# Attention in chunks with a carried state: another order of the chunk's work on four engines, and a state term in four matmuls instead of six

## What is computed

```python
x  = L0_attn_x                                   # 4 x 1024 x 256, float32
xn = layernorm(x)
gammas = 1.0 - 2.0 ** (-5.0 - arange(16))
q, k, v = (xn @ W.T for W in (W_q, W_k, W_v))    # 16 heads of 16
decay = where(i >= j, gammas ** (i - j), 0)
attn  = einsum('bihd,bjhd->bhij', q, k) * decay / 4
y     = einsum('bhij,bjhd->bihd', attn, v)       # then a norm per head, and W_o
...
out = x + attention(xn) + ffn(xn)                # ffn: 8 experts, the best 2 of each token
```

## Time and profile before

| | us |
|---|---|
| median of 3 runs | 962.76 (961.16 to 964.6) |
| the profiled execution, device time | 965.13 |
| its span, first to last instruction | 963.1 |
| mean granted TensorE clock, as a share of full speed | 0.955 |
| busy over the span: TensorE, VectorE, ScalarE, GpSimd | 857.8, 763.6, 573.5, 561.7 |

### The profile page before, as it was taken

The page is one execution under the profiler, slowest core; times in us unless marked ns, Lnnn a source line. Parts: engine busy times, 40 slices in busy tenths (PEclk is TensorE's granted clock), DMA queues, the critical chain, the costliest instruction groups (busy, mean ns, idle before and its releaser), DMA issues.

```text
span 963.1 us, 22162 instructions
## 1 busy us (share of the span) xinstructions
PE 857.8 (89%) x7040; PEld 805.8 (84%) x7040; DVE 763.6 (79%) x1156; ACT 573.5 (60%) x1009; POOL 561.7 (58%) x409
## 2 busy tenths in 40 slices
PE   3949889889888888799899999999999999999865
PEld 1438778778777777699899999999999999999855
DVE  5687877777777778847888888888888888888476
ACT  3824444444443444338677787777777777777541
POOL 2217565666666666535566666666666666666254
PEclk9959999999999999959999999999999999999877
DMA  9923333333333333355577677777677777777487
GB/s 304 354 86 97 92 86 85 80 80 82 85 81 84 85 80 82 85 226 175 191 239 226 227 235 232 227 229 231 228 231 229 230 229 229 229 229 221 140 263 254
DMA packets 106249, 170.49 MB, mean 177 GB/s; under 512 B 30768, under 2 KB 77232, under 8 KB 96240
## 3 DMA queue, kind: packets, MB, share of 16 engines
q1 hardware_dynamic: 99408, 151.49, 51.4%
q0 software_dynamic: 6816, 18.69, 5.2%
HBM read 115.88 MB, written 33.18 MB: 155 GB/s over the span
## 4 chain that ended last, share of the span: by engine, by line
PE 60%; DVE 21%; issue 8%; ACT 3%; DMA 3%; another core or an unknown queue 2%; DVEq 1%; POOL 1%; SPq 0%; ACTq 0%
PE ps L706 23%; PE ps L904 22%; DVE arena_r L1142 5%; PE ps L794 5%; DVE arena_f L1149 4%; PE ps L779 2%; PE ps L889 2%; DMA arena_f<-pair_rows 2%; PE ps L819 1%; PE ps L724 1%; PE ps L762 1%; DVE arena_f L1173 1%; DVE y_stats L1165 1%; ACT arena_r L567 1%
## 5 line engine op out<-in xcount | busy, mean ns | idle before, releaser
L706 PE MATMUL ps<-arena_r 128*128 128x256 f32 (+1 forms) x2256 | 291.7, 285 | 20.1 <-DVE arena_f L1173 18.0
L706 PEld LDWEIGHTS ps<-arena_r 128*128 128x128 f32 x2256 | 277.6, 193 | 26.3 <-issue 24.2
L486 POOL TENSOR_TENSOR arena_r<-arena_f,arena_r 128x2048 fp32r<-128x2048 f32 x39 | 191.5, 4909 | 134.3 <-ACT arena_r L560 134.3
L904 PE MATMUL ps<-arena_r 128*128 128x256 f32 x1872 | 234.0, 285 | 0.8 <-DVE gn_t L1298 0.8
L904 PEld LDWEIGHTS ps<-arena_r 128*128 128x128 f32 x1872 | 230.3, 194 | 0.9 <-issue 0.9
L1235 DVE TENSOR_SCALAR arena_f<-arena_f 128x256 f32<-128x256 f32 x78 | 156.0, 2040 | 1.4
L560 ACT ACTIVATE arena_r<-arena_f 128x2048 fp32r<-128x2048 f32 x78 | 145.5, 1919 | 1.6 <-PE ps L706 1.6
L467 POOL TENSOR_TENSOR arena_r<-arena_f,arena_r 128x512 fp32r<-128x512 f32 x64 | 93.7, 1475 | 57.4 <-ACT arena_r L567 55.7
L819 PE MATMUL ps<-arena_r 128*128 128x128 f32 x1024 | 126.1, 284 | 0.0
L819 PEld LDWEIGHTS ps<-arena_r 128*128 128x128 f32 x1024 | 123.5, 201 | 0.0
L639 ACT ACTIVATE arena_f<-ps,arena_f 128x256 f32<-128x256 f32 x156 | 65.0, 471 | 94.3 <-PE ps L904 73.2
(11 more groups left out here) (141 smaller groups left out, 1060.2 us busy)
## 6 DMA issues: line engine op xcount, KB each, us to landing
arena_f<-w SPq DMA_DIRECT2D x78, 1024.0 KB, 6.0
xs_rows<-spare_rows SPq DMA_DIRECT2D x39, 258.0 KB, 3.3
arena_f<-xs_rows SPq DMA_DIRECT2D x39, 258.0 KB, 2.9
arena_r<-arena_r SPq DMA_DIRECT2D x256, 32.0 KB
pair_chunk<-xn SPq DMA_DIRECT2D x32, 256.0 KB, 2.6
arena_f<-pair_rows SPq DMA_DIRECT2D x16, 512.0 KB, 5.4
arena_f<-b SPq DMA_DIRECT2D x39, 128.0 KB, 4.5
xn<-x SPq DMA_DIRECT2D x8, 512.0 KB, 8.8
```

The lines of the kernel that those rows point to most:

```text
L486: nc.gpsimd.tensor_tensor(w1_r[par][:, 1], w1_raw[par], w1_r[par][:, 0].bitcast(F32), ALU.subtract).then_inc(s["w1_l"], 1)
L706: last = pe.matmul(out_ap, lhs(a), rhs(b), start=start and n == 0, stop=stop and n == 2, **kw)
L904: last = pe.matmul(ps[:, 2 + hp, o * SLOT:(o + 1) * SLOT], w1_r[par][:, a, at:at + P], xs_r[:, b, k * SLOT:(k + 1) * SLOT], start=(m == 0 ...
```

## The change

TensorE begins its round with the scores. The transposes of keys and queries, which were at the head, come after the state sums and the x transposes, and the projection is split in two with the y transposes between. VectorE's `transposed_low(i+1)` moves from the head to behind the third mask, the token low part to between masks, the state sum goes ahead of them; output sum and statistics change places, and so do the values' low part and `keys_and_queries`. ScalarE begins with the transposed tokens; the keys' copy comes before the fourth score's. GpSimd's low part of the state moves from behind the scores and keys to the head. Masks 1 and 3 now wait too, for VectorE's own low part. `across` is written with four matmuls: the high part of the queries by both parts of the state at once (256 columns, into both column sets), and the low part by the high part. SyncE is as it was.

```diff
             def step(i, par):            # GpSimd
+                if within(i - 1, NT):
+
+                    pool.wait_ge(s["st_h"], i)
+                    nc.gpsimd.tensor_tensor(state_r[:, 1], state_f.rearrange("p c i -> p (c i)"),
+                                            state_r[:, 0].bitcast(F32), ALU.subtract).then_inc(s["st_l"], 1)
                 if within(i, NT):
                     for g in (0, 2):
...
-                if within(i - 1, NT):
-
-                    pool.wait_ge(s["st_h"], i)
-                    nc.gpsimd.tensor_tensor(state_r[:, 1], state_f.rearrange("p c i -> p (c i)"),
-                                            state_r[:, 0].bitcast(F32), ALU.subtract).then_inc(s["st_l"], 1)
                 if within(i + 2, NT):
                     chunk_scatter(i + 2, par)
...
             def chunk(i, par):           # ScalarE
                 n, np_ = i + 1, 1 - par
+                if within(i + 2, NT):
+                    m = i + 2
+                    act.wait_ge(s["xt_psum"], m + 1)
+
+                    wait(act, s["q_psum"], m - 1)
+                    nc.scalar.activation(xt[:, par, 0], ps[:, 4, 0:256], ACT.Copy).then_inc(s["xt_h"], 1)
...
                 if within(i, NT):
                     score_high(i, par, 0)
                     score_high(i, par, 1)
-                if within(i + 2, NT):
...
-                if within(i, NT):
                     score_high(i, par, 2)
-                    score_high(i, par, 3)
...
                     nc.scalar.activation(k_r[:, np_, 0], kq_f[:, np_, 0:D], ACT.Copy).then_inc(s["k_h"], 1)
+                if within(i, NT):
+                    score_high(i, par, 3)
...
                 y_bank = ps[:, 7, :].rearrange("p (h s d) -> p h s d", h=H, s=2)
                 for c in range(KC):
-                    last = parts(y_bank[:, c * HP:(c + 1) * HP, 0], lambda a: kq_t[:, par, 1, a, c * P:(c + 1) * P],
-                                 lambda b: state_r[:, b, c * P:(c + 1) * P], c == 0, False, skip_group_check=True)
+                    heads = y_bank[:, c * HP:(c + 1) * HP]
+                    both = state_r[:, :, c * P:(c + 1) * P].rearrange("p s (h d) -> p h s d", h=HP)
+                    pe.matmul(heads, kq_t[:, par, 1, 0, c * P:(c + 1) * P], both, start=(c == 0), stop=False, skip_group_check=True)
+                    last = pe.matmul(heads[:, :, 0], kq_t[:, par, 1, 1, c * P:(c + 1) * P], state_r[:, 0, c * P:(c + 1) * P],
+                                     start=False, stop=False, skip_group_check=True)
...
             def chunk(i, par):           # TensorE
+                if within(i, NT):
+                    scores(i, par)
+                if within(i - 1, NT):
+                    state_sums(i - 1, 1 - par)
+                if within(i + 2, NT):
+                    x_transposes(i + 2, par)
                 if within(i + 1, NT):
                     kq_transposes(i + 1, 1 - par)
-                if within(i, NT):
-                    scores(i, par)
+                if within(i - 1, NT):
+                    inside(i - 1, 1 - par)
                 if within(i + 2, NT):
-                    x_transposes(i + 2, par)
-                if within(i - 1, NT):
-                    state_sums(i - 1, 1 - par)
-                    inside(i - 1, 1 - par)
+                    key_value_projection(i + 2, par)
                 if within(i - 2, NT):
                     y_transposes(i - 2, par)
                 if within(i + 2, NT):
-                    projections(i + 2, par)
+                    query_projection(i + 2, par)
                 if within(i, NT):
                     across(i, par)
...
-                if g % 2 == 0:
-                    wait(dve, s["s_l_pool"], 2 * (i - 1) + g // 2 + 1 if not isinstance(i, int) or i > 0 else 0)
+                low = s["s_l_pool"] if g % 2 == 0 else s["s_l_dve"]
+                wait(dve, low, 2 * (i - 1) + g // 2 + 1 if not isinstance(i, int) or i > 0 else 0)
...
             def chunk(i, par):           # VectorE
+                if within(i, NT):
+                    masked_scores(i, 0)
+                    masked_scores(i, 1)
+                if within(i - 1, NT):
+                    state_sum(i - 1)
+                if within(i + 2, NT):
+                    tokens_low(i + 2, par)
+                if within(i, NT):
+                    masked_scores(i, 2)
                 if within(i + 1, NT):
                     transposed_low(i + 1, 1 - par)
                 if within(i, NT):
-                    for g in range(NB):
-                        masked_scores(i, g)
-                if within(i + 2, NT):
-                    tokens_low(i + 2, par)
-                if within(i, NT):
+                    masked_scores(i, 3)
                     score_low(i, par, 1)
                 if within(i - 1, NT):
                     new_state(i - 1)
                 if within(i, NT):
                     score_low(i, par, 3)
+                if within(i - 1, NT):
+                    output_sum(i - 1, 1 - par)
                 if within(i - 3, NT):
                     output_stats(i - 3)
-                if within(i - 1, NT):
-                    output_sum(i - 1, 1 - par)
+                if within(i + 2, NT):
+                    keys_and_queries(i + 2, par)
                 if within(i + 1, NT):
                     values_low(i + 1, 1 - par)
-                if within(i + 2, NT):
-                    keys_and_queries(i + 2, par)
```

25 lines of the change are left out of this document (12 added, 13 removed).

## The result

The changed kernel takes **1020.67 us** (median of 4 runs, 1020.28 to 1024.65); the kernel before, on the same chip, 963.68 (4 runs, 961.16 to 964.84). The ratio is 1.0604, with a 95% interval of 1.0569 to 1.064: slower by 57 us, where 9 were forecast and the range ended at 1000. The profiled execution took 1024.65 us, its span is 1022.6, and its mean granted clock 0.871 against 0.955.

What follows compares the result with a forecast made beforehand. The bound was taken to be a chain through TensorE and VectorE, 11.07 us a round. 30 x (11.28 - 11.07) = +6.3, +2.5 and -0.3 gave 971.3 us; with 0.7 added, 972, range 962 to 1000.

Steps and rivals of the forecast that it cites:

- The ring: TensorE's scores need query copies, which need VectorE's low part, now behind masks needing the previous scores: 11.28 us a round.
- four links: Landing to scores 0.14 us, scores to first mask 1.35, first mask through low part 3.15, query copies 6.64.
- The front: In chunk 0, x transposes waiting for a token load delay key transposes: scores 1 at 80.1, +2.5 us.
- the clock: Rival, 6%: TensorE's idle time lowers its clock; scores and transposes cost about 1 us more a round, 995 us.
- It then idles 1.9 us in one piece: TensorE ends its round's work by 9.6 us, then idles until the next scores; before, 1.48 us in pieces.
- Against: it still works 9.4 of 11.3: Argument against the clock rival: TensorE is still busy 9.4 of 11.3 us a round.
- The long lag: Rival, 20%: first mask still comes 2.31 us after the scores; a round is 12.24 us, the total 1000.
- Nothing lost: GpSimd's state low part, moved ahead of its score parts, still lets later steps start in time: no cost.
- worth nothing in a round: State term on TensorE, six matmuls to four: 0.2 us saved ahead of idle time, no gain in a round.
- VectorE held by GpSimd: Rival, 3%: the values' low part meets GpSimd's chain and passes the next mask by 0.5 us; 980 us.
- the forecast's signs: If right: score matmuls 11.2 to 11.5 us apart, TensorE idle near 1.9 us, first mask 1.35 us after scores.

Runs made afterwards that it cites:

- the filler: Changed kernel with eight unused matmuls of 512 columns added behind the state term at the end of TensorE's round: 976.32 us.
- the early low part: Changed kernel with key and query transposes right behind the scores, ScalarE's copy of them first, their low part behind two masks instead of three: 938.3 us.
- the kernel with the scatter moved: Kernel before, with one wait added so GpSimd issues its two indirect DMAs only when the round's scores are done: 1025.19 us.
- six matmuls: Changed kernel with the state term written in six matmuls again instead of four: 1055.15 us.

## Why the prediction was wrong

- **The ring: right.** Its four links were put at 0.14, 1.35, 3.15 and 6.64 us, and measured at 0.22, 1.12, 3.16 and 6.71: 11.21 for 11.28. The sum comes this close by some luck. It was made for rounds that all begin behind a wait, and only there is the link from scores to mask the forecast's 1.35 us (1.34 measured); such rounds took 11.41 us with the filler. The 1.12 belongs to rounds that follow a long one without a gap. The ring binds as described, released by the query copies, and the wait of L706 for the output sum is gone.
- **The front: right.** Scores of chunk 1 at 80.03, for the 80.1 of the sum.
- **The step that failed: the clock.** "It then idles 1.9 us in one piece" stood in the forecast with no price in its sum, and the rival that knew better had 6% and 1 us a round. Two things were mis-sized. The idle time was 2.41 us, 0.5 more, since TensorE's work came to 8.80 us a short round where 9.42 had been counted; in part its blocks run into each other now (the key and query transposes, counted at 0.63 us, take 0.36 to the next start, 280.18 to 280.54), and the rest isn't shown. And the price was looked for on the ring alone, where scores and transposes at half clock cost about 1 us. But at half clock TensorE's work no longer fits into the ring: it becomes the bound, and the round is 13.9 to 15.4 us. The forecast had the numbers for it: its own 9.42 us of work would be up to 18.8 at half clock, so as soon as the clock is at half for most of a round, TensorE sets it. With the 51 us of the 14 such rounds the forecast's 971.3 becomes 1022. "Against: it still works 9.4 of 11.3" was no argument: the busy share was as high before, 9.59 of 11.07, but with its idle time in pieces. The eight-matmul filler and the early low part show both sides: with 0.54 or 1.11 us for the wait ahead of the scores the late rounds stayed at full clock, with 1.52 and 2.41 every second one fell. Whether it goes by this wait alone isn't shown: single early rounds fell or held against it.

The Trainium skill has this pattern, in TensorE: Matmul & The Clock Gate, under "HAM oscillation — how this bites in real kernels": a kernel that waits for a DMA once in each tile starts every tile at the lower clock. The trace agrees as to the kind, an alternation driven by a wait for a DMA, with two differences. The scores behind the wait begin at full clock, which fell 0.6 to 2.4 us later (1.9 in the pair shown). And here the slow round needs no DMA in time, so it runs through at 100% busy (13.88 of 13.88 us), and only every second one is slow.

- **The long lag: half right.** The 20% were for a lag of 2.31 us on the ring. In the changed kernel it is 1.12 or 1.34, as forecast. That GpSimd's indirect DMAs make it is now shown (9.96 for 11.07 without them). But the reason given for its absence, that they start behind the first mask, holds only where a long round begins. Where a short one begins, the first one starts ahead of the mask, often the second too, and they hold nothing, as here before the mask at 279.42:

```profile
279.07 0.96 POOL L457 DMA_INDIRECT xs_rows<-pair_chunk,row_chunk  x1 [0.31 <-issue]
```
- **"Nothing lost" for GpSimd's new order, and "worth nothing in a round" for the state term: wrong** in the changed kernel, by 28 and 31 us; the state term's is right in the kernel before (0.34%). Both were costed as work, by whether it lies in idle time, and for GpSimd's order that reading was right: without the indirect DMAs it is worth nothing in the mean round, the state term 0.27 us. What undoing them also did was to bring back the hold of the mask by GpSimd's DMAs; how is open.
- **VectorE held by GpSimd**: not in the changed kernel on the ring (the values' low part behind it takes 1.13 us for 0.41 in the short rounds, in free time), but 3.24 us in the kernel with the scatter moved.
- Of the forecast's signs, the distance of the score matmuls told the failure: only every second one was 11.2 us.

**Open.** Why the same distance between scores and indirect DMA holds the first mask in one kernel and not in another: in the changed kernel, DMAs that begin 0.77 us after the scores (279.07 to 278.30) hold nothing, and with six matmuls ones that begin 0.73 us after them do. What decides it was not found. Nor why the clock fell in one or two early rounds of the kernels that otherwise held it.

## What to carry to other kernels

When a change gathers an engine's scattered idle time into one wait a round, cost the round twice, at full and at half clock: if TensorE's work at half clock exceeds the chain, the clock will set the rounds, and the engine's busy share doesn't tell. Read rounds one by one with their clock, since a mean of 12.96 hid rounds of 11.2 and 15.4. The remedy is to shorten the chain (one block moved forward on each of three engines gave 938 us), and not only to trim the work beside it: the two matmuls less of the state term widened the gap from 2.20 to 2.41 us; and a step is "worth nothing" only if nothing is timed against its end.

## What the runs showed of the hardware that had not been expected

- TensorE at half clock stays there through work without any gap: in the round at 314.59 it is busy for 15.42 of 15.42 us and has a mean clock of 0.56, that is half clock for 13.6 us.
- More work can take less time: 8 unused matmuls of 512 columns a round, 1020.67 to 976.32 us; 3 of them, 1037.53.
- GpSimd's indirect DMAs hold back the moment at which VectorE sees TensorE's scores: in the kernel before, the mask came 2.31 us after the scores in the round shown, 0.70 behind the second DMA, and 1.35 in every round without DMAs; they cost 1.1 us of each round of 11.07. In the changed kernel they hold nothing.
- In rounds of the device loop the 24 score matmuls take 0.98 us when they follow other matmuls without a gap and 1.31 behind a wait of 2.41 us, both at full clock; in a round written out, 0.98 behind 2.32 us of waiting.
- VectorE's subtraction with both inputs in SBUF takes 0.7 us alone and 3.24 beside GpSimd's (2.51 for two).
- Eight small copies take 5.19 us to issue on SyncE, and four take 2.55 on ScalarE, during which ScalarE does nothing else.
